# A recurrent layer and a selective scan on one core: delta from a softplus table, and all loops written out

## The chip, the cores and the metric

The kernel runs on one core of one Trainium2 chip. The core has five engines, each with a queue of its own that it works through in order: PE (TensorE, matrix products into PSUM; its weight loads are listed as PEld), DVE (VectorE), ACT (ScalarE, functions from a table), POOL (GpSimd) and SP (SyncE, which issues the DMAs here). Engines wait for each other by semaphores. The metric is the device time of one execution in microseconds (us).

## What is computed

Two layers with residuals on an image tensor of 32 x 14 x 14 x 384 (196 positions, 384 channels). Only the parts that matter here:

```python
# layer 0: group norm, then a GRU over the 196 positions, then a projection
def step(h, xz):
    h_zrn = h @ Wh.T + bh
    z = sigmoid(x_z + h_z); r = sigmoid(x_r + h_r)
    ncand = tanh(x_n + r * h_n)
    return (1 - z) * ncand + z * h

# layer 1: group norm, in-projection, 3x3 depthwise conv, silu, then four scan directions K=4
x_dbl = einsum('bkdl,kcd->bkcl', xs, x_proj_w)
dts, Bs, Cs = split(x_dbl, [R, R + N], axis=2)          # R = 24, N = 16 states
dts = einsum('bkrl,kdr->bkdl', dts, dt_projs_w)
dts = softplus(dts + dt_projs_b[None, :, :, None])      # this is delta
As  = -exp(A_logs).reshape(K, DI, N)                    # DI = 192
def scan_step(h, inp):
    dA = exp(d_t[..., None] * As)
    h = h * dA + (d_t * u_t)[..., None] * B_t
    y = einsum('bkcn,bkn->bkc', h, C_t)
# sum of the four directions, layer norm, gate with silu(z), out-projection, residual
```

## The kernel before

The program has three stages. **The GRU** (span about 50 to 717 us) makes 196 steps; in each, PE multiplies the state (`h_part`, L1121) and the next input (`x_part`, L1112), ACT makes the gates, DVE mixes them, POOL normalises the next input and keeps the state. **The convolution stage** (719 to about 1003 us) goes over 16 pairs of images: y-projection, group norm, in-projection, nine taps of the convolution on DVE; SP loads `x_in` for a pair and spills three results of it. **The scan stage** (to the end) goes over 16 pairs (`i`), in each over four directions (`st` 0 to 3, in the order `KS = (0, 2, 1, 3)`), and in each direction over 12 groups (`g`) of states. A direction is numbered `P = 4 i + st`; `P1` is the next one.

In one group the work goes round the engines so:

- ACT, `decays` (L963 for g below 8, L967 above): two halves, each writes exp(delta A) into one of three PSUM banks (`DEC = 3`). It waits until the scan three halves earlier is done: ACT is at most three halves, which is one group and a half, ahead of DVE.
- POOL, `drive` (L495): du times B into a ring of six buffers.
- DVE, `scan` (L776 forward, L779 backward), twice, then `read_out` (L788), which multiplies by C; it waits for `c_ready`, which PE's `spread` of the same group gives.
- PE, `spread` (L1234): C over the partitions; it waits for the read-out of the group before. Then `reduce` (L1244) of the group before.

Beside that, each direction prepares the next one's delta, and the order in which this stands is written out by hand in `pair` of each engine. PE makes dt in two parts in PSUM bank 7 (`dt_proj`, at g 0 and g 2; the second waits until ACT has read the first). ACT reads each part twice, as Abs and as Relu (`softplus`, L934 and L935, at g 2 and g 4; each read counts up `dt_read`). Then come the steps of the series for log(1 + exp(-|x|)): on ACT Exp and Square at g 5 (L941, L943) and Copy and Ln at g 6 (L947, L948); on POOL multiply, subtract and add at g 10 (L464, L468, L471); on DVE the choice between series and Ln after group 8 (`choose`, L793); on POOL the sum, which is delta (L477), and du (L482) at g 11.

PE also does the layer norm and the out-projection of the pair before, in bank 7 too: centring at direction 0 (`centre_hw` at g 3, L1259), variance at direction 1 (`var`, g 4 and 6), out-projection and residual at direction 2 (g 6) and direction 3 (g 3 and 5; L1292, L1294, L1299). Since bank 7 must be free, PE's queue has, from pair 1 on, a wait in group 3 of every direction, behind its `spread` and `reduce`: `pe.wait_ge(s["dt_read"], P1 * 4 + 4)`. Everything that follows in PE's queue, the `spread` of group 4 first, stands behind it. Pair 0 has no such wait before group 8.

The steady parts of the three stages are loops on the engines (`Fori`: GRU steps two at a time, pairs 2 to 15 of the convolution stage, pairs 1 to 14 of the scan stage), with counters in registers from which the waits are worked out. The first and last rounds are written out.

Of the kernel before, what the change touches and what calls it, by code (L numbers as in the profile page):

```python
# [14 lines left out]
ALU = mybir.AluOpType  # L15
# [3 lines left out]
T = H * W  # L19
# [7 lines left out]
PAIRS = B // 2  # L27
# [16 lines left out]
SMALL = 0.022  # L44
# [5 lines left out]
def build(nc, x_seq, x_pair, wx, wh, bx, bh, wp, win, par, xproj, dtproj, wout, out):  # L50
# [6 lines left out]
    with ExitStack() as ctx:  # L57
# [35 lines left out]
        series_bias = sb("series_bias", [128, 1])  # L93
# [40 lines left out]
        def carve(cols):  # L134
# [16 lines left out]
        soft = carve(TC)  # L151
        relu = carve(TC)
        lnp = carve(TC)
        poly = carve(TC)
# [26 lines left out]
            "dt_ready", "dt_read", "soft_step", "series_step", "choice_ready", "log_ready", "delta_ready", "du_ready",  # L181
# [49 lines left out]
        def _(sp):  # L231
# [54 lines left out]
            with sp.Fori(2, PAIRS) as i:  # L286
# [75 lines left out]
            with nc.Fori(1, PAIRS - 1, engines=[sp.engine], hint_back_edge=True) as i:  # L362
                pair(i, False, False)
# [6 lines left out]
        def _(pool):  # L370
# [46 lines left out]
            def tok(t):  # L417
                return seq[:, :, bass.ds(t, 1)].rearrange("p c o -> p (c o)") if not isinstance(t, int) else seq[:, :, t]
# [8 lines left out]
            with pool.Fori(0, T // 2 - 1) as i:  # L427
# [16 lines left out]
            with pool.Fori(1, PAIRS) as i:  # L444
                rstd_c(i)
# [14 lines left out]
            def delta_step(n, P, k, b, early=False):  # L460

                if n == 0:
                    pool.wait_ge(s["soft_step"], P * 4 + 3)
                    pool.tensor_tensor(poly, poly, soft, ALU.mult).then_inc(s["series_step"], 1)  # L464
                elif n == 1:
                    pool.wait_ge(s["soft_step"], P * 4 + 4)
                    pool.wait_ge(s["series_step"], P * 2 + 1)
                    pool.tensor_tensor(poly, poly, lnp, ALU.subtract).then_inc(s["series_step"], 1)  # L468
                elif n == 2:
                    pool.wait_ge(s["series_step"], P * 2 + 2)  # L470
                    pool.tensor_tensor(lnp, lnp, relu, ALU.add).then_inc(s["log_ready"], 1)  # L471
                elif n == 3:
                    pool.wait_ge(s["choice_ready"], P + 1)
                    pool.wait_ge(s["log_ready"], P + 1)
                    if not early:
                        pool.wait_ge(s["decay_ready"], (P - 1) * (2 * GRP))
# [961 lines left out]
```

## Time and profile before

| | us |
|---|---|
| median of three runs | 3238.71 (3237.17 to 3238.81) |
| the profiled execution: its own time | 3240.27 |
| its span, first to last instruction | 3238.3 |
| mean granted TensorE clock | 0.991 |
| PE, DVE, ACT, POOL busy | 2779.2, 2672.7, 1824.2, 2243.0 |

The span is read in three stages. In the GRU PE is busy from end to end. In the convolution stage no engine is; the work goes in a ring through SP's loads. In the scan stage DVE is busy 98% of the time, and PE, ACT and POOL wait for it. The profile's slices in tenths show the same: PE at 9 from slice 2 to slice 13, then DVE at 9 from slice 14 on.

### The profile page before, as it was taken

How to read it: one execution, taken by the hardware profiler on the slowest of the kernel's cores; microseconds unless marked ns; L12 is line 12 of the kernel's file. 1: busy time of each engine (PE TensorE's matmuls, PEld its weight loads, DVE VectorE, ACT ScalarE, POOL GpSimd, SP SyncE). 2: the span in 40 equal slices, each digit the busy share in tenths (PEclk: the TensorE clock that was granted, in tenths of full speed). 3: DMA queues.
4: the chain of work that ended last, by engine and by line, in shares of the span. 5: the costliest groups of instructions: out<-in, count | busy, mean ns of one | idle time of the engine just before them, and what ended most of it. 6: DMA issues, size and time to landing. Idle time of an engine off the chain costs nothing.

```text
span 3238.3 us, 101526 instructions
## 1 busy us (share of the span) xinstructions
PE 2779.2 (86%) x39496; PEld 2070.2 (64%) x39496; DVE 2672.7 (83%) x4226; ACT 1824.2 (56%) x3872; POOL 2243.0 (69%) x1878
## 2 busy tenths in 40 slices
PE   4999999999996788888888888888888888888886
PEld 4999999986664555555555555565555655656554
DVE  6444444445776999999999999999999999999995
ACT  1111111112224677777777777777777777777773
POOL 5333333320005989989899898888989898898983
PEclk9999999999997999999999999999999999999999
DMA  5000000002334555545545555455454554555541
GB/s 199 0 0 0 0 0 0 0 5 97 112 112 140 156 156 153 153 156 149 177 140 163 159 144 169 141 160 174 134 170 149 157 163 140 162 161 155 162 146 46
DMA packets 57085, 385.29 MB, mean 119 GB/s; under 512 B 10100, under 2 KB 15060, under 8 KB 31700
## 3 DMA queue, kind: packets, MB, share of 16 engines
q1 hardware_dynamic: 57044, 384.79, 38.8%
q8 instruction: 20, 0.33, 0.0%
q14 instruction: 21, 0.17, 0.0%
HBM read 352.64 MB, written 32.11 MB: 119 GB/s over the span
## 4 chain that ended last, share of the span: by engine, by line
DVE 30%; PE 25%; issue 23%; POOL 16%; ACT 3%; DMA 1%; DVEq 1%; POOLq 0%; SPq 0%; ACTq 0%
DVE arena L776 15%; PE ps L1112 10%; PE ps L1121 9%; POOL arena L495 9%; DVE arena L779 9%; PE ps L1108 2%; DVE arena L793 1%; DVE conv_out L203 1%; POOL arena L471 1%; POOL arena L464 1%; POOL arena L468 1%; DVEq L773 1%; DMA x_in<-x_pair 1%; POOL arena L477 1%; POOL arena L482 1%
## 5 line engine op out<-in xcount | busy, mean ns | idle before, releaser
L1244 PE MATMUL ps<-arena,ident 128*128 128x392 f32 (+1 forms) x4096 | 1163.0, 417 | 0.9 <-DVE arena L788 0.9
L963 ACT ACTIVATE ps<-arena,abias,a 128x390 f32<-128x390 f32 x1024 | 690.0, 677 | 317.4 <-DVE arena L779 179.8
L788 DVE TENSOR_TENSOR arena<-arena,ps 128x784 f32<-128x784 f32 x768 | 745.7, 971 | 38.2 <-PE ps L1234 12.8
L1244 PEld LDWEIGHTS ps<-arena,ident 128*128 128x128 f32 x4096 | 682.8, 191 | 143.9 <-DVE arena L788 1.2
L776 DVE TENSOR_TENSOR_SCAN arena<-ps,arena 128x392 f32<-128x392 f32 x768 | 702.6, 956 | 7.4 <-POOL arena L495 6.3
L779 DVE TENSOR_TENSOR_SCAN arena<-ps,arena 128x392 f32<-128x392 f32 x768 | 702.6, 956 | 0.0
L1234 PE MATMUL ps<-arena,sel 96*128 96x196 bf16 x3072 | 391.6, 250 | 355.7 <-DVE arena L788 355.7
L1234 PEld LDWEIGHTS ps<-arena,sel 96*128 96x128 bf16 x3072 | 227.5, 97 | 665.0 <-DVE arena L788 630.7
L967 ACT ACTIVATE ps<-arena,abias,a 128x195 f32<-128x195 f32 x1024 | 477.7, 505 | 254.2 <-DVE arena L776 139.8
L495 POOL TENSOR_TENSOR arena<-arena 128x784 f32<-128x784 f32 x256 | 472.7, 1851 | 102.6 <-PE ps L1244 97.3
L495 POOL TENSOR_TENSOR arena<-arena,wx_sb 128x784 f32<-128x784 f32 x256 | 465.4, 1850 | 14.4 <-POOL arena L482 13.7
L495 POOL TENSOR_TENSOR arena<-arena,wh_sb 128x784 f32<-128x784 f32 x256 | 467.9, 1850 | 0.0
L422 POOL COPY arena<-h_t 128x96 f32 x196 | 71.6, 365 | 421.5 <-DVE h_t L667 421.5
L1112 PE MATMUL ps<-wx_sb,x_cur 128*32 128x96 f32 x14112 | 333.2, 248 | 0.0
L1121 PE MATMUL ps<-wh_sb,h_t 128*32 128x96 f32 x14112 | 330.6, 247 | 0.0
L1112 PEld LDWEIGHTS ps<-wx_sb,x_cur 128*32 128x32 f32 x14112 | 290.9, 110 | 23.1 <-issue 0.2
L652 DVE TENSOR_TENSOR rh<-r_gate,ps 128x96 f32<-128x96 f32 x196 | 49.8, 254 | 308.6 <-PE ps L1121 308.6
L1121 PEld LDWEIGHTS ps<-wh_sb,h_t 128*32 128x32 f32 x14112 | 296.9, 110 | 4.9
L843 ACT ACTIVATE r_gate<-ps 128x96 f32<-128x96 f32 x196 | 49.0, 250 | 394.0 <-PE ps L1121 394.0
L439 POOL TENSOR_TENSOR grstd<-gsum,neg_half 128x6 f32<-128x6 f32 x16 | 21.2, 1323 | 240.3 <-DVE gsum L723 240.3
L1214 PE MATMUL ps<-arena,bc_w 128*128 128x196 f32 x768 | 150.0, 332 | 1.5 <-ACT arena L935 0.8
L1214 PEld LDWEIGHTS ps<-arena,bc_w 128*128 128x128 f32 x768 | 133.6, 192 | 19.6 <-ACT arena L935 1.4
(175 smaller groups left out, 3295.4 us busy)
## 6 DMA issues: line engine op xcount, KB each, us to landing
wx_sb<-b_by_state SPq DMA_DIRECT2D x64, 1568.0 KB, 6.3
wh_sb<-b_by_state SPq DMA_DIRECT2D x64, 1568.0 KB, 6.3
arena<-b_by_image SPq DMA_DIRECT2D x128, 784.0 KB, 9.1
arena<-x_seq SPq DMA_DIRECT2D x4, 2352.0 KB, 15.9
x_in<-x_pair SPq DMA_DIRECT2D x16, 588.0 KB, 4.2
x_dram<-x SPq DMA_DIRECT2D x16, 588.0 KB, 2.8
x<-x_dram SPq DMA_DIRECT2D x16, 588.0 KB, 10.0
out<-xhat SPq DMA_DIRECT2D x16, 588.0 KB, 2.8
```

Source lines behind the costliest of these rows:

```text
L422: pool.tensor_copy(tok(t), h_t[:, p, :]).then_inc(s["hist_done"], 1)
L495: pool.tensor_tensor(view(hb[(st * GRP + g) % RING]), dux(du[b]), view(src), ALU.mult).then_inc(s["drive_ready"], 1)
L776: dve.tensor_tensor_scan(h, ps[:, bank, 0:HALF_C], h, 0.0, ALU.mult, ALU.add).then_inc(s["scan_done"], 1)
L779: dve.tensor_tensor_scan(h[:, ::-1], ps[:, bank, 1:HALF_C + 1][:, ::-1], h[:, ::-1], 0.0, ALU.mult, ALU.add).then_inc(s["scan_done"], 1)
L788: dve.tensor_tensor(h, h, bank(3), ALU.mult).then_inc(s["readout_ready"], 1)
L963: ins = act.activation(r, src, ACT.Exp, scale=a01[:, c:c + 1], bias=abias01[:, c:c + 1])
L967: ins = act.activation(r[:, m, :], delta[b][:, T2 + lo:T2 + lo + T - 1], ACT.Exp, scale=a2[:, c:c + 1], bias=abias2[:, c:c + 1])
L1112: mm = pe.matmul(ps[32 * j:32 * j + 32, bank + p, 0:CJ], x_cur[:, p, 32 * k:32 * k + 32], wx_sb[:, k, j, lo:lo + CJ], start=False, stop=False)
L1121: mm = pe.matmul(ps[32 * j:32 * j + 32, bank + p, at:at + CJ], h_t[:, 1 - p, 32 * k:32 * k + 32], wh_sb[:, k, j, lo:lo + CJ], start=False, ...
L1214: mm = pe.matmul(ps[:, 7, bc * T:(bc + 1) * T], bc_w[:, k, bc, tile, :], x[:, tile * T:(tile + 1) * T], start=(tile == 0), stop=(tile == 2))
L1234: mm = pe.matmul(ps[:, 3 + m // 2, m % 2 * T:m % 2 * T + T], sel[:, n, kind, :], rhs, start=True, stop=True)
L1244: mm = pe.matmul(ps[:, 5 if g < 8 else 6, 0:cols], ident[:, :], h[:, m * cols:(m + 1) * cols], start=(opens and m == 0), stop=(closes and ...
```

## The change

Delta is made by ACT alone. The second part of dt (196 columns, tile 2) is now made first; ACT keeps it with its bias in `dt2` (`keep_dt2`, at g 2). The larger part (392 columns) is made at g 2 of PE and read at g 5 of ACT: `softplus` loads the softplus table, makes the two pieces of delta with one ACTIVATE each, and loads the table for Exp and Ln back. `dt_read` goes up by two for each direction instead of four. POOL keeps only du (`make_du`, g 11); DVE's `choose` is gone. All `Fori` loops are Python loops, so that every round has instructions of its own with constants.

```diff
-                if n == 0:
-                    pool.wait_ge(s["soft_step"], P * 4 + 3)
-                    pool.tensor_tensor(poly, poly, soft, ALU.mult).then_inc(s["series_step"], 1)
...
+            def make_du(P, k, b, early=False):
+
+                pool.wait_ge(s["delta_ready"], P * 2 + 2)
...
-                        if g == 8 and not (last and st == K4 - 1):
-                            choose(i * K4 + (st + 1))
...
+            def keep_dt2(P, k):
+
+                act.wait_ge(s["dt_ready"], P * 2 + 1)
+                act.wait_ge(s["delta_ready"], P * 2)
+                act.activation(dt2, ps[:, 7, 0:T], ACT.Identity, bias=par2[:, P_DTB + k:P_DTB + k + 1]).then_inc(s["dt_read"], 1)
+
+            def softplus(P, k, b):
+
+                act.preload_act_table_set("softplus")
+                act.wait_ge(s["dt_ready"], P * 2 + 2)
+                act.activation(delta[b][:, 0:T2], ps[:, 7, 0:T2], ACT.Softplus, bias=par01[:, P_DTB + k:P_DTB + k + 1]
+                               ).then_inc(s["dt_read"], 1)
+                act.wait_ge(s["dt_read"], P * 2 + 1)
+                act.activation(delta[b][:, T2:TC], dt2, ACT.Softplus).then_inc(s["delta_ready"], 2)
+                act.preload_act_table_set("natural_log_exp_and_others")
...
                             if g == 2:
-                                softplus(P1, k1, 0)
+                                keep_dt2(P1, k1)
                             if g == 3:
                                 mid_parts(P1, n1)
-                            if g == 4:
-                                softplus(P1, k1, 1)
                             if g == 5:
-                                series(P1, 0)
-                            if g == 6:
-                                series(P1, 1)
+                                softplus(P1, k1, n1 % 2)
...
                         if not head:
                             if g in (3, 4) and ahead:
                                 if st != 3 or g == 3:
-                                    pe.wait_ge(s["dt_read"], P1 * 4 + 4)
+                                    pe.wait_ge(s["dt_read"], P1 * 2 + 2)
...
-            with nc.Fori(1, PAIRS - 1, engines=[pe.engine], hint_back_edge=True) as i:
+            for i in range(1, PAIRS - 1):
                 pair(i, False, False)
```

On ACT, from the second half of group 4 to group 5 in direction 1 of a pair. First before (L963 is a half of `decays`; L934 and L935 are the last two reads of dt; L941 and L943 begin the series):

```order
L963 ACTIVATE ps<-arena,abias,a 128x2x195 [waits scan_done]
L934 ACTIVATE arena<-ps,par 128x196 [waits dt_ready]
L935 ACTIVATE arena<-ps,par 128x196
L959 REGISTER_ALU
L963 ACTIVATE ps<-arena,abias,a 128x2x195 [waits scan_done]
L959 REGISTER_ALU
L963 ACTIVATE ps<-arena,abias,a 128x2x195 [waits scan_done]
L940 ISA
L941 ACTIVATE arena<-arena 128x588 [waits dt_read]
L942 REGISTER_ALU
L943 ACTIVATE arena<-arena,series_bias 128x588 [waits soft_step]
```

and now, from group 4 on (L923 is a half of `decays`, the four halves of groups 4 and 5 in one row; L968 is the variance's Ln of the pair before, behind group 6):

```order
L923 ACTIVATE ps<-arena,abias,a 128x2x195 [waits scan_done] x4
L901 ACT_TABLE_LOAD
L903 ACTIVATE arena<-ps,par 128x392 [waits dt_ready]
L906 ACTIVATE arena<-arena 128x196 [waits dt_read]
L907 ACT_TABLE_LOAD
L923 ACTIVATE ps<-arena,abias,a 128x2x195 [waits scan_done] x2
L968 ACTIVATE arena<-ps 128x392 [waits var_ready]
```

The two reads that end `dt_read`'s count stood behind the halves of group 4; now the last of them is the first ACTIVATE behind the table load, behind the halves of group 5.

On PE, groups 3 and 4 of the same direction: before (L1234 `spread`, L1244 `reduce`, L1259 to L1261 `var`; the first REGISTER_ALU row carries the wait for `dt_read`),

```order
L1234 MATMUL ps<-arena,sel 128x196 [waits readout_ready]
L1234 MATMUL ps<-arena,sel 128x196 x3
L1244 MATMUL ps<-arena,ident 128x392 x2
L1329 REGISTER_ALU
L1313 REGISTER_ALU [waits dt_read]
L1234 MATMUL ps<-arena,sel 128x196 [waits readout_ready]
L1234 MATMUL ps<-arena,sel 128x196 x3
L1244 MATMUL ps<-arena,ident 128x392 x2
L1259 MATMUL ps<-arena,avg 128x392 [waits ysq_ready,dt_read]
L1260 MATMUL ps<-arena,avg 128x196
L1261 MATMUL ps<-arena,avg 128x196
```

and now (L1187 `spread`, L1197 `reduce`, L1212 to L1214 `var`):

```order
L1187 MATMUL ps<-arena,sel 128x196 [waits readout_ready]
L1187 MATMUL ps<-arena,sel 128x196 x3
L1197 MATMUL ps<-arena,ident 128x392 x2
L1187 MATMUL ps<-arena,sel 128x196 [waits readout_ready,dt_read]
L1187 MATMUL ps<-arena,sel 128x196 x3
L1197 MATMUL ps<-arena,ident 128x392 x2
L1212 MATMUL ps<-arena,avg 128x392 [waits ysq_ready,dt_read]
L1213 MATMUL ps<-arena,avg 128x196
L1214 MATMUL ps<-arena,avg 128x196
```

Nothing moved on PE: the wait for `dt_read` stands where it stood, between the `reduce` in group 3 and the `spread` of group 4. What has moved is what it waits for.

## Rows read from the trace of the kernel before

**Rows 1.** windows of whole stages: length, busy us of each engine, PEclk, DMA share

```profile
55.00:715.00 660.00, 660.00 (x28498) 604.24 (x28492) 285.41 (x1163) 130.26 (x582) 216.66 (x580) 1.00 0.00 0
...
1022.80:3204.00 2181.20, 1816.79 (x9241) 1257.17 (x9241) 2141.78 (x2367) 1589.99 (x3041) 1952.28 (x1238) 1.00 0.51 154
```

**Rows 2.** groups of DVE instructions by line in the scan stage: xcount, busy, mean ns, idle

```profile
L788 DVE TENSOR_TENSOR arena<-arena,ps 128x784 f32<-128x784 f32 x762 | 739.8, 971 | 38.0 <-PE ps L1234 12.8
...
L793 DVE SCALAR_TENSOR_TENSOR arena<-arena 128x588 f32<-128x588 f32 x63 | 59.4, 943 | 0.0
```

**Rows 3.** DVE in time, direction 1 of a pair: start, length, line; groups 4 and 5

```profile
2024.01 0.97 DVE L788 TENSOR_TENSOR arena<-arena,ps 128x784 f32<-128x784 f32 x1
2024.90 1.83 DVE L779 TENSOR_TENSOR_SCAN arena<-ps,arena 128x392 f32<-128x392 f32 x2
2026.76 0.97 DVE L788 TENSOR_TENSOR arena<-arena,ps 128x784 f32<-128x784 f32 x1
```

**Rows 4.** ACT in time, before the scan stage

```profile
1009.02 1.28 ACT L1065 ACT_TABLE_LOAD   x1
1010.31 0.69 ACT L941 ACTIVATE arena<-arena 128x588 f32<-128x588 f32 x1
...
1013.42 0.32 ACT L920 ACTIVATE arena<-ps 96x196 bf16<-96x196 f32 x1
```

**Rows 5.** ACT in time, the direction of Rows 3; last idle and its releaser

```profile
2015.51 0.57 ACT L934 ACTIVATE arena<-ps,par 128x392 f32<-128x392 f32 x1
...
2023.15 0.68 ACT L963 ACTIVATE ps<-arena,abias,a 128x390 f32<-128x390 f32 x1 [0.74 <-DVE arena L779]
```

**Rows 6.** PE in time, the first groups of the stage

```profile
1025.69 0.83 PE L1234 MATMUL ps<-arena,sel 96*128 96x196 bf16 x4 [10.98 <-DVE arena L788]
1026.31 2.87 PE L1244 MATMUL ps<-arena,ident 128*128 128x392 f32 x4
1028.98 0.66 PE L1234 MATMUL ps<-arena,sel 96*128 96x196 bf16 x4
```

**Rows 7.** PE in time, the direction of Rows 3, groups 3 to 5

```profile
2019.88 1.51 PE L1244 MATMUL ps<-arena,ident 128*128 128x392 f32 x4
...
2023.98 0.82 PE L1259 MATMUL ps<-arena,avg 128*128 128x392 f32 x2
...
2025.30 0.50 PE L1234 MATMUL ps<-arena,sel 96*128 96x196 bf16 x4
```

**Rows 8.** PE in time, group 3 of direction 0

```profile
1987.90 0.92 PE L1259 MATMUL ps<-arena,centring 128*128 128x392 f32 x2 [0.59 <-ACT arena L935]
...
1989.32 0.50 PE L1234 MATMUL ps<-arena,sel 96*128 96x196 bf16 x4
```

**Rows 9.** PE in time, group 3 of direction 3

```profile
2089.92 0.93 PE L1292 MATMUL ps<-arena,wout 128*128 128x392 f32 x2 [0.50 <-ACT arena L935]
...
2092.01 0.50 PE L1234 MATMUL ps<-arena,sel 96*128 96x196 bf16 x4
```

**Rows 10.** windows late in the scan stage, columns as in Rows 1

```profile
3163.00:3166.40 3.40, 1.56 (x11) 1.26 (x10) 3.37 (x5) 1.92 (x5) 3.24 (x3) 0.95 1.09 236
3166.40:3169.80 3.40, 3.40 (x15) 3.08 (x14) 3.37 (x4) 2.20 (x4) 3.40 (x3) 0.55 0.90 192
```

**Rows 11.** PE in time in the GRU: steps 1, 194 and 195

```profile
55.13 1.67 PE L1121 MATMUL ps<-wh_sb,h_t 128*32 128x96 f32 x72
...
712.42 1.67 PE L1121 MATMUL ps<-wh_sb,h_t 128*32 128x96 f32 x72
...
715.80 1.67 PE L1121 MATMUL ps<-wh_sb,h_t 128*32 128x96 f32 x72
```

**Rows 12.** the queue of SP in the convolution stage

```profile
851.86 0.33 SPq L270 DMA_DIRECT2D z_dram<-z_out  x1
852.71 0.35 SPq L266 DMA_DIRECT2D x_in<-x_pair  x1
```

**Rows 13.** DVE in time, start of the scan stage

```profile
1022.79 1.84 DVE L776 TENSOR_TENSOR_SCAN arena<-ps,arena 128x392 f32<-128x392 f32 x2 [6.29 <-POOL arena L495]
```

More of the change, by code:

```diff
@@ L285, in _ @@
             spill_z(0)
-            with sp.Fori(2, PAIRS) as i:
+            for i in range(2, PAIRS):
                 load_x(i)
@@ L426, in _ @@
             norm(1, 1, True)
-            with pool.Fori(0, T // 2 - 1) as i:
+            for i in range(0, T // 2 - 1):
                 for p in range(2):
@@ L443, in _ @@
             rstd_c(0)
-            with pool.Fori(1, PAIRS) as i:
+            for i in range(1, PAIRS):
                 rstd_c(i)
@@ L509, in _ @@
             low_parts(0, 0)
-            for n in range(5):
-                delta_step(n, 0, 0, 0, True)
+            make_du(0, 0, 0, True)
             def pair(i, head, last):
@@ L530, in pair @@
                             low_parts(P1, n1)
-                        if g >= 10:
-                            for n in (0, 1, 2) if g == 10 else (3, 4):
-                                delta_step(n, P1, k1, n1 % 2, head and st == 0)
+                        if g == 11:
+                            make_du(P1, k1, n1 % 2, head and st == 0)
             pair(0, True, False)
-            with nc.Fori(1, PAIRS - 1, engines=[pool.engine], hint_back_edge=True) as i:
+            for i in range(1, PAIRS - 1):
                 pair(i, False, False)
@@ L757, in _ @@
             norm_and_convolve(1, True)
-            with dve.Fori(2, PAIRS) as i:
+            for i in range(2, PAIRS):
                 norm_and_convolve(i)
@@ L802, in pair @@
                         read_out(st, g, G)
-                        if g == 8 and not (last and st == K4 - 1):
-                            choose(i * K4 + (st + 1))
-            choose(0)
             pair(0, True, False)
-            with nc.Fori(1, PAIRS - 1, engines=[dve.engine], hint_back_edge=True) as i:
+            for i in range(1, PAIRS - 1):
                 pair(i, False, False)
@@ L847, in step @@
                 act.activation(cand[:, :], cand_pre[:, :], ACT.Tanh).then_inc(s["tanh_ready"], 1)
-            with act.Fori(0, T // 2) as i:
+            for i in range(0, T // 2):
                 for p in range(2):
@@ L896, in _ @@
             normalise(2)
-            with act.Fori(3, PAIRS) as i:
+            for i in range(3, PAIRS):
                 conv_silu(i - 2)
@@ L1071, in _ @@
             pair(0, True, False)
-            with nc.Fori(1, PAIRS - 1, engines=[act.engine], hint_back_edge=True) as i:
+            for i in range(1, PAIRS - 1):
                 pair(i, False, False)
@@ L1137, in step @@
                     x_part(1 - p)
-            with pe.Fori(0, T // 2 - 1) as i:
+            for i in range(0, T // 2 - 1):
                 for p in range(2):
@@ L1199, in _ @@
             project(1, True)
-            with pe.Fori(2, PAIRS) as i:
+            for i in range(2, PAIRS):
                 project(i)
@@ L1392, in dram @@
 def dram(t, i):
[L1393 removed]
+    return t[i]
 def flat(t):
```

90 lines of the change are left out of this document (21 added, 69 removed).

## The prediction, made before the changed kernel had run

> **What bounds the kernel now.** I read the windows of whole stages first, then the DVE groups by line, then each engine in time over two directions of one pair. In the GRU PE is busy for all of 660.00 us [rows 1]: a step costs what PE needs, and little else counts. In the scan stage, 1022.80 to 3204.00, DVE is busy 2141.78 of 2181.20 us [rows 1]; in all of it DVE waited 12.8 us for PE's `spread` before L788 [rows 2] and for nothing else worth a line. So the scan stage is DVE's instruction list: a group takes 2.75 us (2024.01 to 2026.76), each instruction starting about 0.08 before the one ahead has ended (2024.01 + 0.97 against 2024.90) [rows 3]. Whatever leaves DVE's list is gained in full; whatever makes DVE wait is lost in full. The other engines have slack, but it is counted in groups: ACT is held by `decays` to one and a half groups ahead of DVE, and PE to one `spread`.
>
> **Part 1, the choice on DVE goes.** 63 instructions of 0.943 us stand in the stage [rows 2], each costs 0.943 - 0.08: 63 x 0.86 = 54 us gained. On POOL four of five steps per direction go, and on ACT two reads and the four series steps; both engines wait for DVE or PE today, so that is worth nothing by itself. Hidden by DVE it stays hidden.
>
> **Part 2, the table loads on ACT.** A load takes 1.28 us and the next ACTIVATE starts 0.01 after its end (1009.02, 1010.31) [rows 4]. The block at group 5 is: load 1.28, ACTIVATE of 392 columns out of PSUM 0.57 (L934, 2015.51, the same operands with another function [rows 5]), ACTIVATE of 196 columns about 0.36 (no row of this form; L920 with 196 columns out of PSUM took 0.32 [rows 4], so 0.3 to 0.4), load 1.28, gaps 0.07: 3.6 us. The Softplus function itself shows in no row; I take the 0.57 of L934, with twice that as the other end.
>
> The Trainium skill (ScalarE: Activation LUTs, What ACT_TABLE_LOAD costs) adds a drain of about 1380 ns to every switch, some 2.66 us in all. The trace shows no such drain behind the load: 0.01. By the page the release worked out in part 3 would come 1.4 later in each of 59 directions, an estimate of 81 us more; I go by the row.
>
> **Part 3, what the wait in PE's queue now waits for.** This carries the forecast. From pair 1 on PE stops in group 3 until `dt_read` is complete, with the `spread` of group 4 behind it. Before, that was the last read at ACT's group 4. Now it is the ACTIVATE behind the load, at ACT's group 5. In the same direction: the last half of `decays` before it starts at 2023.15, released by DVE's scan of group 4 [rows 5], and takes 0.68; nothing can move it earlier. Then load and ACTIVATE: 2023.83 + 0.01 + 1.28 + 0.01 + 0.57 = 2025.70, and PE starts 0.1 later, 2025.80. DVE's read-out of group 4 starts at 2024.01 [rows 3] and needs that `spread`, which comes 0.61 before a read-out that waits for it (0.51 long and 0.10 to get there; cold 0.83 + 0.10 [rows 6]). So it can start at 2026.41 at best: 2.4 us late. The work that frees PE hangs on DVE's own scan of group 4, so no pace of any other engine hides this.
>
> The four directions differ by what PE has behind the wait. Let R be PE's restart; before a read-out is due there are 0.86 from 2023.15 to 2024.01, in each direction alike. Of PE's own pieces: `reduce` 2.67 cold (1026.31 to 1028.98 [rows 6]), half of it, 1.34, warm; `var` and `centre_wh` 1.32 (2023.98 to 2025.30 [rows 7]); `centre_hw` 1.42 and then `spread` (1987.90 to 1989.32 [rows 8]); out-projection and residual 2.09 (2089.92 to 2092.01 [rows 9]). **With a warm PE** read-out 4 is late by 2.4 in directions 1 and 2. In direction 1 `reduce` and `var` come before the next `spread`, R + 0.35 + 1.34 + 1.32 + 0.61 = R + 3.6 against R + 0.61 + 2.75: 0.3 more, 2.7. In direction 0, where `centre_hw` stands first, 2.4 + 1.4, plus 0.3 at group 5 less the 0.3 that DVE loses there today: 3.8. In direction 3 2.4 + 2.1 less the 0.6 lost today: 3.9. (Those losses are the 12.8 of [rows 2].) Sum 12.8 us for a pair; 15 pairs, less the last direction of the last pair, which prepares nothing: 188 us.
>
> **But PE will not be warm.** In direction 1 `reduce` ends at 2021.39 [rows 7] and PE restarts at 2025.80: 4.4 us idle, in every direction of 15 pairs. Late in the stage one window in which PE was busy 1.56 of 3.40 us, with the clock still at 0.95 of full speed, was followed by one at 0.55, 2.4 GHz down to 1.2 [rows 10]; and after the 10.98 us of idle before 1025.69 `spread` took 0.83 instead of 0.51 and `reduce` 2.87 instead of 1.51 [rows 6, 7]. That slow stretch ended between 1028.98 and the warm rows behind it, some 4 us after the restart. I take 5 us at 1.2 GHz after each R. Then a group costs PE 0.62 + 2.67 = 3.3 us, more than DVE's 2.75. Direction 1: read-out 4 at R + 0.93, 2.7 late; `reduce` until R + 3.3, `var` until R + 5.5 (part of it warm), read-out 5 at R + 6.1 against R + 3.7: 2.4 more, 5.1. Direction 2: 2.7, and read-out 5 at R + 4.2 against R + 3.7: 3.3. Direction 0: `centre_hw` 2.8, read-out 4 at R + 3.7, 5.5 late; then `reduce`, `centre_wh` and `spread` until R + 7.5 against R + 6.5, less today's 0.3: 6.2. Direction 3: 4.2 for the projection, read-out 4 at R + 5.1, less today's 0.6: 6.3. Sum 20.9 for a pair, x 15 - 6.3 = 307 us.
>
> In pair 0 no wait stands at group 3; there only ACT's block counts. It ends at 2023.83 + 3.6 = 2027.4 in the frame of [rows 5], the next half 0.68 later, and the scan that needs it, due at 2027.65, starts at 2028.2: 0.55 x 4 = 2 us. In the other pairs that is covered by DVE's own lateness.
>
> **Part 4, the loops.** GRU: from step 1 to step 194 a step takes (712.42 - 55.13) / 193 = 3.406 us, the one that is written out already, 712.42 to 715.80, 3.38 [rows 11]: 194 x 0.026 = 5 us gained. Convolution stage: SP issues the load of `x_in` 0.85 after the spill of z (851.86, 852.71), of which 0.33 is the issue itself [rows 12]; up to 0.5 over 14 rounds is 0 to 7, I take 5 gained. Scan stage: no gain, since DVE does not wait for a register; pair 0 and pair 15 are straight code already and no slower. **The start of the scan stage** loses the chain of series, choice and POOL steps. DVE's first scan is at 1022.79, after 6.29 us of waiting for POOL [rows 13]. Now delta is there 3.6 after a load that starts some 3 us earlier than 1009.02, and ACT's last piece before `decays`, L920, ended at 1013.74 [rows 4]; a half of `decays` later, 0.7, DVE can start, near 1014: 9 us gained.
>
> **Sum**, on the profiled span: 3238.3 - 54 + 307 + 2 - 5 - 5 - 9 = 3474.3. The execution's own time lay 2.0 above its span and 1.6 above the median of the three runs: about **3475 us**, 7% slower.
>
> **Rivals.** (a) *The clock holds.* If idle of 4.4 us does not bring PE down, part 3 costs 188: 3356 us. For it: elsewhere in the stage PE idles 0.9 us in each group at full clock. Against it: [rows 10], where less idle was enough. 15%. (b) *PE stays slow longer*, about 10 us after each restart: with 3.3 us a group against 2.75 and the late extras of directions 0 and 3, about 3 us more per direction, 59 x 3 = 177: 3650 us. 8%. (c) *Written-out code starves PE in the GRU.* A step is 147 matmuls with as many weight loads in 3.4 us, and code that is not looped must be brought in all the time. The straight steps at 712.42 and 715.80 show no stall, but they are two, not 196. The Trainium skill (Runtime: NRT & Kernel Launch, Instruction fetch mechanics) says that the next block is fetched while the current one runs, and calls this mostly hidden: by the page (c) has no price. Should a tenth of a step show, which is an assumption between the 0 of the straight steps and no known upper end, it costs 196 x 0.34 = 67 us: 3540 us. 12%. (d) *The other side, faster*: the `spread` of group 4 is not held, because ACT's block comes early enough, and only parts 1 and 4 are left: 3238 - 54 - 19 + 2, about 3170 us. It decides at the release: dt must be read before 2023.4, that is 2.3 us earlier than worked out, and ACT would have to stand a group further ahead than three PSUM banks let it. If the loads were not executed where they stand, the release is still at 2024.5, and most of the loss stays. 5%.
>
> **How the numbers follow.** Forecast 58%, (a) 15, (b) 8, (c) 12, (d) 5, the rest for mishaps on either side. The range leaves out (b) and (d) and most of the rest: 3345 to 3590; its lower end is (a), the upper end takes in (c) and a cold stretch of 7 instead of 5 us. 0.2% is about what a measurement of this kernel can tell from no change: faster by more than that 6%, within it 2%, slower 92%.
>
> **What would show it.** L788's idle grows from 38.0 us to over 300, put down to `spread`, one long wait at group 4 of each direction from pair 1 on and none in pair 0; PE idle 4.4 us there, released by ACT's Softplus; a mean granted clock near 0.9 over a pair instead of 1.00 (with (a) 1.00); L793 gone; GRU steps at 3.38 us (with (c) PE idle on "issue" inside steps); ACT_TABLE_LOAD at 1.28 and nothing behind it. I am wrong at the root if read-out 4 starts on time.

## The result, and the profile of the changed kernel

The changed kernel takes **3639.61 us** (median of 4 runs, 3637.82 to 3644.73) against 3238.19 before: ratio 1.1243, 95% interval 1.1223 to 1.1262. The prediction was 3475, range 3345 to 3590: the right direction, but 165 us too little and outside the range. The profiled execution has a span of 3636.9 us, 398.6 more than before. Cut at three events that both traces have, it divides like this (us):

| stretch | before | after | change | forecast |
|---|---|---|---|---|
| start to the last `h_part` (GRU) | 717.5 | 878.3 | +160.9 | -5 |
| to the last convolution instruction on DVE | 286.1 | 285.4 | -0.6 | -5 |
| to the first scan | 19.3 | 10.0 | -9.3 | -9 |
| to the end (scan stage) | 2215.5 | 2463.1 | +247.6 | -54 + 307 + 2 = +255 |

So three lines came within 8 us of their forecast (the convolution stage's 5 did not show), and the GRU's has the wrong sign. Start with that one. The page's slices of the changed kernel (40 slices of 91 us: PE's busy share in tenths, its granted clock in tenths, GB/s of all DMA; then the queue that brings instructions):

```profile
PE   5888888888997778878878788787787877887876
...
PEclk9999999999998999999989999899999999999999
...
GB/s 179 5 5 5 5 5 5 5 5 21 112 107 134 164 157 123 148 142 129 147 125 146 158 120 149 131 142 146 129 142 145 130 143 146 133 138 145 132 136 59
...
q8 instruction: 309, 5.06, 0.6%
```

PE's nines in the GRU have become eights, and where the DMA traffic was 0 it is 5 GB/s: the queue of instructions, 309 packets where the kernel before had 20. The same stretch as in [rows 1], with columns as there:

```profile
55.00:715.00 660.00, 580.35 (x22984) 501.84 (x22977) 229.78 (x936) 104.78 (x468) 164.12 (x471) 1.00 0.02 5
```

PE is busy 580.35 of 660.00 us, where it had been busy for all of it, at full clock. PE in time, early in the GRU (start, length, line; in brackets the idle time ahead):

```profile
60.37 2.06 PE L1065 MATMUL ps<-wx_sb,x_cur 128*32 128x96 f32 x71
...
64.29 0.52 PE L1074 MATMUL ps<-wh_sb,h_t 128*32 128x96 f32 x10 [0.61 <-issue]
...
65.01 1.69 PE L1065 MATMUL ps<-wx_sb,x_cur 128*32 128x96 f32 x72
...
68.02 0.86 PE L1074 MATMUL ps<-wh_sb,h_t 128*32 128x96 f32 x29 [0.34 <-issue]
...
71.75 1.20 PE L1074 MATMUL ps<-wh_sb,h_t 128*32 128x96 f32 x48 [0.48 <-issue]
```

The gaps cut through the 72 matmuls of one `h_part` (10, 29, 48 of them are left behind the gap). All 72 wait for the same data, so data can't stop PE after the 62nd; and "issue" says that nothing in the profile released it. What is left behind the gap grows by 19 from step to step, so 147 - 19 = 128 matmuls lie between two gaps, with their weight loads 256 instructions. Over the whole run 51.7 and 43.3 us of "issue" stand before the GRU's two groups of matmuls, 95 of the 160.9; the rest shows as groups that are stretched, as the `x_part` of 2.06 above beside one of 1.69. Between 100 and 800 the instruction queue of the changed kernel carried

```profile
q8 instruction: 190, 3.11, 1.8%
```

3.11 MB in 190 packets, 16 KB each, on average one in 700 / 190 = 3.68 us, each busy only about a third of that. A step has 147 matmuls and as many weight loads, 294 instructions. Taken as 64 bytes each, 256 fill a packet (the run e5 below bears it out: 221 more packets of 16 KB for 194 x 294 instructions, 63.5 bytes each). 294 / 256 x 3.68 = 4.23 us for a step; measured (878.3 - 717.5) / 194 more than 3.41, that is 4.24. That the two agree shows only that each instruction is brought in once; that the packets set the pace, and not PE the packets, is what the gaps say and what e5 and e7 test.

The scan stage is what the prediction had drawn. DVE in time in direction 1 of a pair, the same place as [rows 3]:

```profile
2278.69 0.97 DVE L763 TENSOR_TENSOR arena<-arena,ps 128x784 f32<-128x784 f32 x1
2279.58 1.83 DVE L754 TENSOR_TENSOR_SCAN arena<-ps,arena 128x392 f32<-128x392 f32 x2
2284.16 0.97 DVE L763 TENSOR_TENSOR arena<-arena,ps 128x784 f32<-128x784 f32 x1 [2.75 <-PE ps L1187]
2285.04 1.83 DVE L754 TENSOR_TENSOR_SCAN arena<-ps,arena 128x392 f32<-128x392 f32 x2
2289.52 0.97 DVE L763 TENSOR_TENSOR arena<-arena,ps 128x784 f32<-128x784 f32 x1 [2.65 <-PE ps L1187]
```

Read-out 4 is 2.75 us late, read-out 5 another 2.65; forecast 2.7 and 2.4. ACT and PE of the same moment show why; they answer to [rows 5] and [rows 7]:

```profile
2280.58 0.68 ACT L923 ACTIVATE ps<-arena,abias,a 128x390 f32<-128x390 f32 x1 [1.21 <-DVE arena L754]
2281.28 1.28 ACT L901 ACT_TABLE_LOAD   x1
2282.57 0.59 ACT L903 ACTIVATE arena<-ps,par 128x392 f32<-128x392 f32 x1
2283.06 0.36 ACT L906 ACTIVATE arena<-arena 128x196 f32<-128x196 f32 x1
2283.43 1.28 ACT L907 ACT_TABLE_LOAD   x1
```

```profile
2283.22 0.83 PE L1187 MATMUL ps<-arena,sel 96*128 96x196 bf16 x4 [4.40 <-ACT arena L903]
2283.84 2.87 PE L1197 MATMUL ps<-arena,ident 128*128 128x392 f32 x4
2286.51 1.51 PE L1212 MATMUL ps<-arena,avg 128*128 128x392 f32 x2
...
2288.91 0.50 PE L1187 MATMUL ps<-arena,sel 96*128 96x196 bf16 x4
```

The load takes 1.28 and the function's ACTIVATE starts 0.01 after its end and lasts 0.59; PE, idle for 4.40, restarts 0.06 after that and is slow: `spread` 0.83, `reduce` 2.87. The windows of that moment, columns as in [rows 1]:

```profile
2275.70:2279.10 3.40, 2.88 (x12) 1.21 (x10) 3.33 (x5) 2.55 (x6) 1.98 (x2) 1.00 0.17 33
2279.10:2282.50 3.40, 0.00 (x0) 0.00 (x0) 2.31 (x3) 2.17 (x3) 2.26 (x2) 0.91 0.88 317
2282.50:2285.90 3.40, 2.68 (x8) 1.70 (x9) 1.74 (x2) 2.87 (x5) 0.00 (x0) 0.50 0.29 122
2285.90:2289.30 3.40, 3.40 (x13) 2.38 (x12) 0.97 (x2) 0.87 (x2) 1.85 (x1) 0.59 0.00 0
2289.30:2292.70 3.40, 3.40 (x17) 2.15 (x16) 3.14 (x4) 1.99 (x4) 1.86 (x2) 1.00 0.01 2
```

Granted clock 1.00, then 0.91 with PE idle, 0.50 (1.2 GHz) and 0.59 after the restart, 1.00 (2.4 GHz) again. Over the whole stage the DVE group that answers to L788 of [rows 2] is

```profile
L763 DVE TENSOR_TENSOR arena<-arena,ps 128x784 f32<-128x784 f32 x768 | 745.6, 971 | 342.4 <-PE ps L1187 320.0 <-DVE arena L751 0.5
```

320.0 us waiting for `spread`, 307.2 more than the 12.8 of before; the forecast was 307. The stage as a whole lost 7 less than the 255 forecast: 2.8 behind DVE's last instruction (31.6 instead of 34.4), 1.1 of stops on "issue" at the start and the exit of DVE's loop, 3.0 in small gaps before the read-outs, which the prediction had put at nothing.

### The profile page after: what moved, and what is told of

The parts are those of the page before. It is cut to its first block, busy times and chain, and to the rows that moved or that the text cites. A ratio compares the mean times of both kernels' runs of the same rounds, so it can differ in the third digit from the quotient of the medians.

```text
span 3636.9 us, 92428 instructions
## 1 busy us (share of the span) xinstructions
PE 2955.1 (81%) x39496; PEld 2176.0 (60%) x39496; DVE 2616.6 (72%) x4161; ACT 1809.3 (50%) x3679; POOL 1877.2 (52%) x1622
## 4 chain that ended last, share of the span: by engine, by line
PE 38%; DVE 32%; issue 23%; ACT 6%; DMA 0%; POOL 0%; POOLq 0%; DVEq 0%; ACTq 0%; SPq 0%
DVE arena L754 15%; DVE arena L751 14%; PE ps L1065 10%; PE ps L1074 9%; PE ps L1197 5%; PE ps L1187 2%; ACT L901 2%; PE ps L1118 2%; DVE conv_out L198 2%; PE ps L1212 2%; PE ps L1061 1%; PE ps L1245 1%; PE ps L1247 1%; PE ps L1252 1%; ACT arena L903 1%
## 5 line engine op out<-in xcount | busy, mean ns | idle before, releaser
L1197 PE MATMUL ps<-arena,ident 128*128 128x392 f32 (+1 forms) x4096 | 1216.1, 431 | 0.9 <-DVE arena L763 0.9
L763 DVE TENSOR_TENSOR arena<-arena,ps 128x784 f32<-128x784 f32 x768 | 745.6, 971 | 342.4 <-PE ps L1187 320.0
L923 ACT ACTIVATE ps<-arena,abias,a 128x390 f32<-128x390 f32 x1024 | 693.6, 678 | 549.5 <-DVE arena L754 280.5
L1197 PEld LDWEIGHTS ps<-arena,ident 128*128 128x128 f32 x4096 | 708.0, 198 | 160.9 <-issue 29.5
L1187 PE MATMUL ps<-arena,sel 96*128 96x196 bf16 x3072 | 413.4, 260 | 369.9 <-DVE arena L763 228.9
L1187 PEld LDWEIGHTS ps<-arena,sel 96*128 96x128 bf16 x3072 | 247.7, 102 | 670.0 <-DVE arena L763 386.3
L1074 PE MATMUL ps<-wh_sb,h_t 128*32 128x96 f32 x14112 | 370.6, 247 | 52.9 <-issue 51.7
L1065 PE MATMUL ps<-wx_sb,x_cur 128*32 128x96 f32 x14112 | 366.1, 249 | 44.4 <-issue 43.3
L1074 PEld LDWEIGHTS ps<-wh_sb,h_t 128*32 128x32 f32 x14112 | 319.9, 110 | 76.6 <-issue 76.6
L1065 PEld LDWEIGHTS ps<-wx_sb,x_cur 128*32 128x32 f32 x14112 | 301.1, 110 | 90.3 <-issue 67.7
L417 POOL COPY arena<-h_t 128x96 f32<-128x96 f32 x196 | 71.1, 363 | 540.4 <-DVE h_t L642 540.4
L811 ACT ACTIVATE z_gate<-ps 128x96 f32<-128x96 f32 x196 | 49.0, 250 | 202.7 <-PE ps L1074 202.7
## 6 DMA issues: line engine op xcount, KB each, us to landing
x<-x_dram SPq DMA_DIRECT2D x16, 588.0 KB, 10.4
```

Of the source, the lines that this page charges most:

```text
L763: dve.tensor_tensor(h, h, bank(3), ALU.mult).then_inc(s["readout_ready"], 1)
L923: ins = act.activation(r, src, ACT.Exp, scale=a01[:, c:c + 1], bias=abias01[:, c:c + 1])
L1065: mm = pe.matmul(ps[32 * j:32 * j + 32, bank + p, 0:CJ], x_cur[:, p, 32 * k:32 * k + 32], wx_sb[:, k, j, lo:lo + CJ], start=False, stop=False)
L1074: mm = pe.matmul(ps[32 * j:32 * j + 32, bank + p, at:at + CJ], h_t[:, 1 - p, 32 * k:32 * k + 32], wh_sb[:, k, j, lo:lo + CJ], start=False, ...
L1187: mm = pe.matmul(ps[:, 3 + m // 2, m % 2 * T:m % 2 * T + T], sel[:, n, kind, :], rhs, start=True, stop=True)
L1197: mm = pe.matmul(ps[:, 5 if g < 8 else 6, 0:cols], ident[:, :], h[:, m * cols:(m + 1) * cols], start=(opens and m == 0), stop=(closes and ...
```

## The experiments

Theory: two losses that have nothing to do with each other. *GRU:* PE's written-out steps need instructions faster than they arrive. *Scan stage:* dt is read behind a table load, PE stands behind that wait, and comes out of it with a slow clock. Rivals: that written-out code as such, on all engines, costs time, in the scan stage too; that the wait alone makes the scan stage's loss; that a fixed stall at each block of code, not the rate, makes the GRU's; that what DVE waits for is set by the slow PE and not by the release.

e1, e4 and e8 were run four times, the others once; repeated runs of one kernel lay within about 0.3%, some 10 us. All runs made from the changed kernel use the stand-in of e1 for the softplus table and function.

| kernel | us | against |
|---|---|---|
| e1 changed kernel, loops as before | 3488.6 | 3639.6 |
| e3 changed kernel, PE's GRU loop alone put back | 3472.1 | 3639.6 |
| e5 kernel before, PE's GRU loop alone written out | 3403.3 | 3238.2 |
| e6, e7 longer step; looped, written out | 3791.9, 3787.1 | each other |
| e9, e10 loop body of 4 and of 8 steps | 3240.4, 3510.2 | 3238.2 |
| e2, e12 as e1, PE kept at work before the wait (32, 48 matmuls) | 3384.9, 3376.1 | 3488.6 |
| e11 as e1, one more table load | 3570.7 | 3488.6 |
| e4 as e1, dt read ahead of the load | 3196.2 | 3238.2 |
| e8 as e3, dt read ahead of the load | 3189.0 | 3238.2 |

### The two losses apart

**e1_softplus_loops**, all loops put back:

```diff
-            for i in range(0, T // 2 - 1):
-                for p in range(2):
-                    step(i * 2 + p, p)
+            with pe.Fori(0, T // 2 - 1) as i:
+                for p in range(2):
+                    step(i * 2 + p, p)
...
-                act.preload_act_table_set("softplus")
+                act.preload_act_table_set("sigmoid_and_others")
```

> The changed kernel with every loop as it was before: only the way to delta is changed. For the table function a stand-in is used in its place, ACT.Sigmoid with its own table, so delta is another number; instructions, waits, table loads and sizes are the same. Theory: the GRU's 160.6 us come from the written-out code alone, and the scan stage's 247.6 us (1173.77 to 3602.5 in the changed kernel, against 2181.1 before) from the wait behind dt_read alone. Then the last h_part ends near 717.5 again, the scan stage stays at 2429 and the time is 3639.6 - 161 + 1 = 3479 us (3470 to 3490). Rival: part of the scan stage's loss too comes from written-out code; then the scan stage is clearly shorter than 2429 and the time below 3460. A scan stage at 2429 also shows that the stand-in costs what the function it stands for costs.

Ratio to the kernel before 1.0770 (1.0752 to 1.0788). The last `h_part` ends at 717.4: the GRU's loss is gone, all of it. From the first scan to the end 2473.2 us pass, 10 more than in the changed kernel, not fewer. So the rival is out, and the stand-in is as costly as the function: the same waits, L763 idle 340.9 against 342.4, 153.6 us a pair in both. Of the 10 us, 3.0 lie behind DVE's last instruction, and 6.7 are one stop of DVE, at the exit of its loop over pairs (DVE in time):

```profile
3329.73 0.97 DVE L763 TENSOR_TENSOR arena<-arena,ps 128x784 f32<-128x784 f32 x1
3337.40 1.84 DVE L751 TENSOR_TENSOR_SCAN arena<-ps,arena 128x392 f32<-128x392 f32 x2 [6.70 <-issue]
```

**e3_pe_gru_looped**: of the edit above, only the stand-in and PE's loop over the GRU.

> The changed kernel, all written out, with one loop put back: PE's loop over the GRU's steps. The stand-in of ACT.Sigmoid again, so delta is another number. Theory: PE alone is starved of instructions in the GRU (294 instructions a step), the written-out code of DVE, ACT and POOL costs nothing: last h_part near 717.5, total 3639.6 - 161 = 3479 us (3468 to 3490). Rival: the written-out steps of the other engines (some 20 instructions a step on each) share in the loss through the waits that a step makes between engines: then a step stays above 3.5 us, the total above 3500.

The last `h_part` ends at 715.9, so PE's own code is the whole loss; the steps written out on DVE, ACT and POOL cost nothing (1.5 us less than in e1). From the first scan on 2462.5 us, within 0.6 of the changed kernel: the scan stage needs no loop on any engine. About half of the 7 us under the expectation lies in the convolution stage, 282.1, the shortest of all runs (the others 284.5 to 291.6, with loops and without, so the 5 us that the prediction gave to it are not to be told from the scatter).

**e5_before_pe_gru_out**: the reverse, in the kernel before.

```diff
-            with pe.Fori(0, T // 2 - 1) as i:
+            for i in range(0, T // 2 - 1):
```

> The kernel before with one edit: PE's loop over 194 steps of the GRU written out. Theory: PE's instructions come in one packet of 16 KB every 3.69 us, that is 256 instructions of 64 bytes, and a step has 294: 294 / 256 x 3.69 = 4.24 us a step instead of 3.41, 194 x 0.83 = 161 us; less the 1.5 that PE's straight code may give: 3399 us (3385 to 3405). Rival: in the changed kernel the loss needed the other engines' written-out code too, whose fetches share the same queue: then 3240 to 3370.

3403.3, and the last `h_part` ends at 882.9, 165.4 later. One loop makes the loss, on a kernel without any table load. Its groups of PE by line show the idle put down to "issue":

```profile
L1121 PE MATMUL ps<-wh_sb,h_t 128*32 128x96 f32 x14112 | 370.7, 247 | 55.4 <-issue 54.5
L1112 PE MATMUL ps<-wx_sb,x_cur 128*32 128x96 f32 x14112 | 366.2, 249 | 46.4 <-issue 45.7
```

### A rate, or a stall at each block

**e6_pace_looped** and **e7_pace_written_out** make the recurrence slower on DVE, so that PE needs its 294 instructions less often:

```diff
                 dve.wait_ge(s["hnat_ready"], t + 1)
+                for n in range(2):
+                    dve.memset(xhat[:, :, :], 0.0).then_inc(s["held"], 1)
+                    dve.wait_ge(s["held"], t * 2 + (n + 1))
```

> The kernel before, with two memsets of xhat (1176 columns, each waited for) on DVE in every GRU step between h_nat and its transpose; nothing else reads them then. This only gives the recurrence a longer step, some 2 to 2.6 us more if all of it is on the path: 3630 to 3750 us, a step of 5.4 to 6.0. It is the partner of the next run.

> The same two memsets a step, and PE's GRU loop written out. Theory (a rate): code arrives at 16 KB per 3.69 us, enough for a step of 4.24 us; a step that lasts over 5 us for another reason is not slowed: the same as with the loop within 15 us. Rival (a stall at each block): each of the 228 blocks costs PE its 0.7 us whatever the pace: 161 us more than with the loop.

3791.9 and 3787.1: with a step of (1262.0 - 55) / 195 = 6.2 us the written-out steps cost nothing, though the same 241 blocks are brought in. PE's `wx` group, which had 45.7 us on "issue" in e5, has 1.0 here:

```profile
L1115 PE MATMUL ps<-wx_sb,x_cur 128*32 128x96 f32 x14112 | 368.8, 262 | 1.2 <-issue 1.0
```

So it is no fixed stall at each block, it is a rate: at 294 instructions in 3.4 us PE wants code faster than the 256 in 3.68 us that it got, and is late; at 294 in 6.2 us nothing shows. No run lies between the two. e6 itself came out 42 us above its expectation: the memsets take 1.04 each and 0.31 for each wait, 2.7 in all on the path, and the slower steps let the clock fall now and then (0.90 over the GRU).

### How long a loop may be

**e9_body_of_4**, **e10_body_of_8**:

```diff
-            with pe.Fori(0, T // 2 - 1) as i:
-                for p in range(2):
-                    step(i * 2 + p, p)
+            for t in range(2):
+                step(t, t)
+            with pe.Fori(0, (T - 4) // 4) as i:
+                for q in range(4):
+                    step(i * 4 + (q + 2), q % 2)
```

> The kernel before with another body of PE's GRU loop: 48 rounds of 4 steps (1176 matmuls and weight loads) in place of 97 rounds of 2 (588), two steps written out ahead. In the kernel before the body of 588 is not fetched again: 20 instruction packets in the whole run. Theory (a body that fits is kept, and 1176 still fits): 3238 us, a step of 3.41, some 20 to 30 packets. Rival (what is kept ends between 588 and 1176): code comes again in each round at 3.69 us a packet, as with written-out steps: 3395 to 3405 us and over 200 packets. The Trainium skill (Runtime: NRT & Kernel Launch, Instruction fetch mechanics) states two lines of 16 KiB for an engine's instructions; by that already the body of 588 (36.75 KB) would not be kept, which 20 packets contradict.

> The same with 24 rounds of 8 steps (2352 matmuls and weight loads, 147 KB). Theory: it no longer fits, code comes again in each round and PE is starved as with written-out steps: 3395 to 3405 us, over 200 packets. Rival (what is kept is larger, or a loop is fetched at another pace): 3238 us.

A body of 1176 instructions (75 KB) is kept: 3240.4 us and no packet at all between 100 and 700. A body of 2352 (150 KB) isn't, and is dearer than no loop, 3510 against 3403: besides the gaps inside steps, each of the 23 jumps back has a stop of 3.3 to 3.8 us, 81 us in all. PE in time at such a jump:

```profile
399.74 1.69 PE L1112 MATMUL ps<-wx_sb,x_cur 128*32 128x96 f32 x72
405.04 2.82 PE L1121 MATMUL ps<-wh_sb,h_t 128*32 128x96 f32 x72 [3.60 <-issue]
```

and it is slow behind it (2.82 instead of 1.69, at a granted clock of 0.59 from 404.80 to 408.20). The expectation of e10 missed this by 105 us. The Trainium skill (Runtime: NRT & Kernel Launch, Instruction fetch mechanics) gives PE 128 KiB of instruction memory in one sentence and "only 2 cache lines" of 16 KiB in another. The expectation of e9 went by the second alone; the two runs agree with the first. The Trainium skill's rule, in the same section, that a taken jump out of what is held must fetch before it can go on agrees with the 3.60.

### What the scan stage's loss is made of

**e2_warm_pe**; in **e12_warm_48** the 32 is 48:

```diff
                             if g in (3, 4) and ahead:
+                                if g == 3:
+                                    for _ in range(32):
+                                        pe.matmul(ps[:, 5, 0:T], sel[:, 0, 0, :], bcs[st][0:96, :], start=False, stop=False)
                                 if st != 3 or g == 3:
                                     pe.wait_ge(s["dt_read"], P1 * 2 + 2)
```

> As the kernel with loops and the stand-in, and PE does 32 matmuls of 196 columns (operands of spread) in group 3, before its wait for dt_read, in each direction of pairs 1 to 15. They add to the sums of bank 5, so the output is another one. Nothing that DVE waits for stands behind them but what stood behind the wait anyway. At the 0.13 us of a matmul of spread (0.51 for 4) they fill 4 of the 4.4 us that PE is idle there. Theory: the scan stage's loss is the wait, 188 us, plus a cold PE after it; with PE busy the clock stays at full speed and 188 is left: 3238 - 54 - 9 + 188 = 3363 us (3350 to 3390), granted clock over 0.98 in the scan stage. Rival: the wait alone makes the loss and the lower clock is only its companion: as without the matmuls, near 3479.

e2 got 104 us of the expected 125. Its 32 matmuls took 2.86 us and left PE idle for 1.77, and whether the clock outlived that differs from place to place. The waits of pairs 1 to 15 end in 59 restarts of PE. Behind 44 of them every matmul is as fast as before the wait, behind 15 (12 of them in direction 2) some are slow. One of each kind, both from direction 1, where the second is the only slow one of 15:

```profile
1200.21 0.51 PE L1187 MATMUL ps<-arena,sel 96*128 96x196 bf16 x4 [1.77 <-ACT arena L903]
1200.55 1.51 PE L1197 MATMUL ps<-arena,ident 128*128 128x392 f32 x4
...
2075.26 2.86 PE L1283 MATMUL ps<-arena,sel 96*128 96x196 bf16 x32
2079.89 0.83 PE L1187 MATMUL ps<-arena,sel 96*128 96x196 bf16 x4 [1.77 <-ACT arena L903]
2080.51 2.81 PE L1197 MATMUL ps<-arena,ident 128*128 128x392 f32 x4
```

The window around the second restart, columns as in [rows 1]:

```profile
2079.90:2083.30 3.40, 3.40 (x9) 2.12 (x10) 2.47 (x3) 2.66 (x4) 0.00 (x0) 0.52 0.03 11
```

So e2 had made its case for the most part, and the expectation of e12, which says of e2 that "the clock still fell", goes by the second kind alone. L763 waits 216.5 us for `spread` in e2, against 318.2 in e1 and 205.9 in e12.

> As the run with 32 matmuls ahead of PE's wait (sums of bank 5 changed, stand-in ACT.Sigmoid), now with 48. There 32 took 2.86 us and left 1.77 idle, and the clock still fell: 0.52 from 2079.90 to 2083.30, spread 0.83 after the wait. 48 take 4.29 of the 4.63. Theory: without an idle stretch the clock stays, spread after the wait takes 0.51, and only the wait is left: from the prediction's terms before - 54 - 9 + 188, plus the 6.7 at the exit of DVE's loop and 3 at the end that the looped runs showed: 3238.2 - 54 - 9 + 188 + 10 = 3373 us (3366 to 3380), granted clock 1.00 between the pairs' groups. Rival: the clock falls at the wait whatever PE did before it: 3385 or more, as with 32.

3376.1, 3 us from the expectation. PE and DVE in the same place of e12:

```profile
2072.56 4.21 PE L1283 MATMUL ps<-arena,sel 96*128 96x196 bf16 x48
2077.20 0.51 PE L1187 MATMUL ps<-arena,sel 96*128 96x196 bf16 x4 [0.43 <-ACT arena L903]
2077.54 1.51 PE L1197 MATMUL ps<-arena,ident 128*128 128x392 f32 x4
```

```profile
2077.81 0.97 DVE L763 TENSOR_TENSOR arena<-arena,ps 128x784 f32<-128x784 f32 x1 [2.49 <-PE ps L1187]
...
2080.82 0.97 DVE L763 TENSOR_TENSOR arena<-arena,ps 128x784 f32<-128x784 f32 x1 [0.29 <-PE ps L1187]
```

`spread` 0.51, `reduce` 1.51, granted clock 1.00 from 2076.50 to 2079.90: the clock held, and read-outs 4 and 5 are late by 2.49 and 0.29, together 2.8 where the prediction's warm case had 2.7. Behind all 59 restarts of e12 the matmuls are fast. The wait alone costs what is left, and the clock cost 3488.6 - 3376.1 = 112 us, by the only difference between e1 and e12 (the waits for `spread` differ by as much, 112.3); the prediction's two cases lie 119 apart. The two were timed on different chips: beside e12 the kernel before took 3244.3 us, beside e1 3238.2, so the 112 is sure to some 6 us.

**e11_two_loads**: `act.preload_act_table_set` ahead of the other load.

> As the kernel with loops and the stand-in (ACT.Sigmoid; delta is another number), with one more table load ahead of the load in each direction. It makes dt_read 1.28 us later and costs nothing else. Theory (the loss is the lateness of dt_read, counted in full, and the slow clock after the idle): 59 directions x 1.28 = 76 us more, 3488.6 + 76 = 3564, up to 20 more where the longer idle makes the slow stretch longer or pair 0's cover of 3.6 us too short (4 x 1.3 = 5): 3560 to 3590 us. Rival (what DVE waits for after group 4 is set by the pace of the cold PE, not by the release): part of the 76 is hidden, under 3540.

82 us more. L763 waits 395.9 us for `spread` instead of 318.2, that is 77.7 / 59 = 1.32 in each direction for a load of 1.28; another 5.9 are waits of DVE for `decays`, 16.3 instead of 10.4. The lateness of the release counts in full, one for one; that the cold PE sets the pace is out. It also prices a table switch anew: the estimate by the Trainium skill's page (ScalarE: Activation LUTs, What ACT_TABLE_LOAD costs) of some 2.66 us would have shown 157 us here.

### A way out

**e4_early_read**: ACT copies dt out of PSUM without a load, where the last read stood before the change, and takes the function over all 588 columns later.

```diff
+            def keep_dt01(P, k):
+                act.wait_ge(s["dt_ready"], P * 2 + 2)
+                act.activation(dtb[:, 0:T2], ps[:, 7, 0:T2], ACT.Identity, bias=par01[:, P_DTB + k:P_DTB + k + 1]
+                               ).then_inc(s["dt_read"], 1)
...
-                act.wait_ge(s["dt_ready"], P * 2 + 2)
-                act.activation(delta[b][:, 0:T2], ps[:, 7, 0:T2], ACT.Sigmoid, bias=par01[:, P_DTB + k:P_DTB + k + 1]
-                               ).then_inc(s["dt_read"], 1)
-                act.wait_ge(s["dt_read"], P * 2 + 1)
-                act.activation(delta[b][:, T2:TC], dt2, ACT.Sigmoid).then_inc(s["delta_ready"], 2)
+                act.wait_ge(s["dt_read"], P * 2 + 2)
+                act.activation(delta[b], dtb, ACT.Sigmoid).then_inc(s["delta_ready"], 2)
...
+                            if g == 4:
+                                keep_dt01(P1, k1)
```

> Loops as before, stand-in of ACT.Sigmoid (delta is another number), and one thing moved: ACT copies both parts of dt out of PSUM, bias added, at groups 2 and 4 (Identity, no table load), which completes dt_read where it was completed before the change; one ACTIVATE of 588 columns from SBUF follows at group 5 between the two table loads. Theory: what costs the time is that dt is read behind a load; with it read ahead, PE does not stand still and the clock holds. 3238 - 54 - 9 = 3175, and up to 15 us for ACT's block of about 3.4 us: 3190 us (3172 to 3210), L763 idle below 60 us, granted clock over 0.98. Rival: the block of two loads is itself too long for ACT's lead of one and a half groups, DVE waits for decays after it in each of 63 directions: with 1 us each 3240, with 2 us 3300.

3196.2 us, ratio 0.9869 (0.9852 to 0.9885): 1.3% faster than the kernel before, with both table loads where they were. DVE's groups by line:

```profile
L763 DVE TENSOR_TENSOR arena<-arena,ps 128x784 f32<-128x784 f32 x768 | 745.8, 971 | 39.6 <-PE ps L1193 12.8
```

The wait for `spread` is the 12.8 us of [rows 2] again. The block on ACT (PE does not appear in it):

```profile
2028.30 0.59 ACT L902 ACTIVATE arena<-ps,par 128x392 f32<-128x392 f32 x1
...
2031.05 1.28 ACT L907 ACT_TABLE_LOAD   x1
2032.34 0.69 ACT L909 ACTIVATE arena<-arena 128x588 f32<-128x588 f32 x1
2033.05 1.28 ACT L910 ACT_TABLE_LOAD   x1
```

3.3 us from load to `decays`, and DVE waits less than 0.2 at a time for the latter: ACT's lead covers the two loads. What cost e1 292 us more (3488.6 against 3196.2) was not the loads but what stood behind them. That holds for the stand-in; this order was not run with the softplus table itself, for which only e3 shows that the stand-in costs the same.

**e8_early_read_out**: e4's edit in e3's kernel.

> dt read ahead of the load as in the run with the early read (stand-in ACT.Sigmoid, so delta is another number), and all loops written out but PE's over the GRU. Writing out the others was worth 3488.6 - 3472.1 = 16.5 us with the late read: 6.7 of it one stop of DVE at the exit of its loop over pairs, 4.0 in the convolution stage, 1.5 in the GRU. Expected: 3196.2 - 16 = 3180 us (3174 to 3188). Rival: the written-out code of PE in the scan stage, where it now never idles for long, is starved there too: over 3200.

3189.0 (3184.5 to 3194.4), ratio 0.9847 (0.9830 to 0.9863), the fastest of all. The rival is out: nothing starves in the scan stage. Of the 16 us only 7 came, and the two intervals overlap, so writing out the rest is a small gain at best. DVE's stop at the loop's exit is gone, but DVE now waits some 0.2 us for `decays` in every direction, 12.1 us in all against 1.3 in e4: here ACT's lead does not quite cover the two loads.

## Why the prediction was wrong

- **The failed step: part 4, the GRU's line, "194 x 0.026 = 5 us gained".** It measured 160.9 us lost. It took a written-out step to be as fast as the two that were written out already [rows 11]. Two steps are no measure for 194 in a row: in the changed kernel too the `h_part` at 55.12 and the one at 58.50 take 1.67 us each, and what follows is late. The trace of before held the number that should have warned: PE busy 660.00 of 660.00, 28,498 matmuls and nearly as many weight loads [rows 1], 86 instructions per us without a pause. What it did not hold is the rate at which code comes: no run of code had to be brought in at such a pace.
- **Rival (c)** named the mechanism, place and sign ("PE idle on issue inside steps"), and was priced at a tenth of a step on no row; it is a quarter, 0.83 of 3.41. With 161 lost in place of 5 gained the sum would be 3474.3 + 166 = 3640.3, against a span of 3636.9 and a median of 3639.6. Its 12% leaned on the Trainium skill's "mostly hidden" (Runtime: NRT & Kernel Launch, Instruction fetch mechanics). The runs bound it: fetching is hidden at 294 instructions in 6.2 us (e7), and not at 294 in 3.4 (e5).
- **Part 1**, 54: DVE's busy time from the first scan on fell from 2141.79 to 2087.77, 54.0.
- **Part 2**: load 1.28, gap 0.01, function 0.59 instead of 0.57; block 3.45 instead of 3.6. That the price of Softplus itself was in no row did no harm. e11 confirms the choice of the row over the page.
- **Part 3**: the mechanism is right, and so are the parts to within 0.8 us. The release comes where worked out, PE idles 4.40 us. Late per direction, forecast against measured, less what was lost there before (0.29, 0.61): direction 0 6.2 against 5.4, 1 5.1 against 5.4, 2 3.3 against 3.5, 3 6.3 against 6.6; sum 20.9 in both, but that the sums agree so closely is luck: direction 0 was too dear by what the others were too cheap. The warm case of 12.8 is 13.1 in e12. Rivals (a) and (b) are out: the clock fell, and was back some 5 us after the restart. In pair 0 DVE waits 0.34 per direction instead of 0.55. What else the stage gave, 7 us, is told above.
- **Start of the scan stage**: 10.0 from the last convolution instruction instead of 19.3, as forecast.
- **Rival (d)**, the side "faster", was sound in its condition: reading dt before the load gives it, as e4 does, 3196 against "about 3170". The changed kernel did not meet it: dt is read 2.4 us too late.

## What to carry to other kernels

Before a loop is written out, divide its instructions by its time: PE got no more than about 70 instructions in a microsecond (256 in 3.68) out of straight code. It starved where it wanted 86, within three steps, and did not at 47; between the two nothing was measured. Keep such loops; on PE a body of 1176 instructions was kept and one of 2352 was not. When a table load is put on an engine, ask which reads stand behind it and who waits for those: with the read ahead of the load, the loads cost DVE 1.3 us in e4 and 12.1 in e8, instead of hundreds.

## What the runs showed that was not expected

- Instructions for written-out code arrive in packets of 16 KB, on average every 3.68 us (3.3 to 4.4 from one to the next), though the packet itself takes about 1.1 and the other queues carry next to nothing. It isn't the queue's limit: in e10 two packets start 1.0 to 2.0 us apart at each of the 23 jumps back. What sets the 3.68, a delay of each fetch or something else, was not settled.
- A loop body that isn't kept costs more than straight code: 23 jumps back with stops of 3.3 to 3.8 us.
- The exit of DVE's loop over pairs cost 6.70 us in e1 and e12, 6.42 in e2 and 6.21 in e4, 0.88 in the kernel before. Why was not tested.
- Matmuls of 2.86 us ahead of 1.77 us of idle kept the clock behind 44 of 59 restarts and lost it behind 15 (e2); in direction 1, with the same rows ahead, 14 restarts are fast and one is slow. With 4.21 us of them and 0.43 idle it held behind all 59 (e12).
